# First attention of a five-block decoder: scores transposed, maxima carried as a row of the score product, sums and division moved behind the weighing of the values

## What is computed

```python
q = einsum('bsd,hdk->bhsk', x, w_q)        # 16 heads, head width 64; k and v alike
scores = einsum('bhqk,bhmk->bhqm', q, k) / 8
weights = softmax(scores, axis=-1)          # rows of 1024
z = einsum('bhqm,bhmk->bhqk', weights, v)
z = z.transpose(0, 2, 1, 3).reshape(b, s, 1024) @ w_o
x = layernorm(x + (x + z))
```

## Time and profile before

| | |
|---|---|
| median of three runs | 2817.43 us |
| profiled execution, its time | 2820.84 us |
| profiled execution, its span | 2819.0 us |
| PE busy | 2588.2 us, 92% of the span |
| DVE busy | 1811.0 us, 64% |
| ACT busy | 1525.7 us, 54% |
| POOL busy | 313.3 us, 11% |
| granted TensorE clock, mean | 0.959 |
| PE in the chain that ended last | 82% |

### The profile page before, as it was taken

One profiled execution on the slowest core, in us unless ns is written; L12 is line 12 of the kernel. 1 busy time (PEld: TensorE's weight loads), 2 busy tenths in 40 slices (PEclk: granted clock), 3 DMA queues, 4 the chain that ended last, 5 costly groups with the idle time before them and its releaser, 6 DMA issues.

```text
span 2819.0 us, 41456 instructions
## 1 busy us (share of the span) xinstructions
PE 2588.2 (92%) x16256; PEld 1902.5 (67%) x16256; DVE 1811.0 (64%) x3522; ACT 1525.7 (54%) x2551; POOL 313.3 (11%) x195
## 2 busy tenths in 40 slices
PE   7999999899999979899999999997999999986662
PEld 6666666766666668788888888996555555554421
DVE  4777774477777554777533444346887777847978
ACT  5777775477777624344444444442666555642332
POOL 0000000000000050101210222001110000004323
PEclk9999999999999989899999999998999999997886
DMA  2000000000000020000100010003222222201000
GB/s 69 16 20 12 16 20 1 19 14 22 12 12 20 1 95 18 31 1 15 47 10 22 31 43 1 8 1 74 65 65 65 65 65 61 61 2 39 1 1 30
DMA packets 47474, 82.37 MB, mean 29 GB/s; under 512 B 9512, under 2 KB 28336, under 8 KB 47280
## 3 DMA queue, kind: packets, MB, share of 16 engines
q1 hardware_dynamic: 47136, 79.65, 11.0%
q10 hardware_dynamic: 144, 0.07, 0.0%
HBM read 36.44 MB, written 2.10 MB: 14 GB/s over the span
## 4 chain that ended last, share of the span: by engine, by line
PE 82%; DVE 12%; ACT 2%; issue 2%; POOL 1%; DMA 1%; SPq 0%; DVEq 0%; ACTq 0%
PE PS L85 71%; PE PS L362 9%; DVE m_gl L921 2%; DVE s_nm L1347 1%; DVE x_E L1746 1%; DVE x_rd L1730 1%; DVE st_s L229 1%; DVE x_sm L1751 1%; DVE X L268 1%; POOL f_H L1952 1%; ACT a_KH L404 0%; PE PS L1803 0%; DMA a_wr<-in_w_v 0%; PE PS L698 0%; DVE f_w L1317 0%
## 5 line engine op out<-in xcount | busy, mean ns | idle before, releaser
L921 DVE TENSOR_TENSOR m_gl<-m_g,m_gh 128x512 fp32r<-128x512 f32 x288 | 258.1, 902 | 386.5 <-ACT m_g L760 386.5
L757 ACT ACTIVATE m_gh<-PS,cols 128x512 fp32r<-128x512 f32 x288 | 198.4, 689 | 469.9 <-PE PS L85 469.9
L483 DVE TENSOR_REDUCE a_nm<-PS 128x1 f32<-128x1024 f32 x256 | 313.5, 1225 | 210.0 <-PE PS L85 207.9
L1347 DVE TENSOR_REDUCE s_nm<-PS 128x1 f32<-128x512 f32 x512 | 344.8, 688 | 70.8 <-PE PS L85 68.2
L426 ACT ACTIVATE a_PT<-PS 128x512 f32<-128x512 f32 x512 | 278.2, 595 | 138.4 <-PE PS L362 136.7
L1264 ACT ACTIVATE s_P<-PS 128x1024 f32<-128x1024 f32 x256 | 262.0, 1024 | 164.7 <-PE PS L85 164.1
L85 PE MATMUL PS<-m_w2h,m_gh 128*128 128x256 f32 x1152 | 324.9, 282 | 18.8 <-DVE m_gl L921 18.6
L85 PE MATMUL PS<-m_w2l,m_gh 128*128 128x256 f32 x1152 | 323.5, 281 | 0.0
L85 PE MATMUL PS<-m_w2h,m_gl 128*128 128x256 f32 x1152 | 323.3, 281 | 0.0
L434 ACT ACTIVATE a_P<-PS,a_nm 128x1024 f32<-128x1024 f32 x256 | 286.1, 1117 | 16.0 <-DVE a_nm L483 15.8
L362 PEld LDWEIGHTS PS<-ident,a_P 128*128 128x128 f32 x2048 | 220.7, 141 | 96.4 <-issue 93.1
(11 more groups left out here) (295 smaller groups left out, 4441.7 us busy)
## 6 DMA issues: line engine op xcount, KB each, us to landing
m_raw<-in_m_w SPq DMA_DIRECT2D x16, 1024.0 KB, 5.1
s_Q<-s_T SPq DMA_DIRECT2D x128, 128.0 KB, 2.4
s_K<-s_T SPq DMA_DIRECT2D x128, 128.0 KB, 2.4
a_KH<-a_KH SPq DMA_DIRECT2D x56, 128.0 KB, 2.3
a_wr<-in_w_qk SPq DMA_DIRECT2D x16, 256.0 KB, 2.9
X<-in_x SPq DMA_DIRECT2D x4, 512.0 KB, 6.3
a_wr<-in_w_v SPq DMA_DIRECT2D x8, 256.0 KB, 2.7
m_raw<-in_c_w SPq DMA_DIRECT2D x2, 1024.0 KB, 8.8
```

What stands on the lines that cost most here:

```text
L483: e.tensor_reduce(a_nm[:, m:m + 1], PS[:, SB[t % 2]:SB[t % 2] + 2, :], AX.XY, ALU.max, negate=True).then_inc(s["a_max"], 1)
L757: e.activation(m_gh[r][:, :], PS[:, 4 + n % 3, :], func, bias=cols[:, bcol:bcol + 1]).then_inc(s["m_gh"], 1)
L921: e.tensor_tensor(m_gl[r][:, :], m_g0[r][:, :], m_gh[r][:, :].bitcast(F32), ALU.subtract).then_inc(s["m_gl"], 1)
L1347: e.tensor_reduce(nm2[:, n % 2, i, half:half + 1], PS[:, half, :], AX.X, ALU.max, negate=True).then_inc(s["s_nr"], 1)
```

## The change

- **Layout.** The scores are computed transposed: 128 keys stationary, 1024 queries moving. The exponentials then lie with the keys on the partitions, which is how the weighing of the values reads them, so the transposes and `a_PT` go. The weighing takes the exponentials of one tile of keys for all 1024 queries: two products of 512 columns a turn, eight turns (one head) into bank 6.
- **Maxima.** They must be known before the transposed scores. A natural product (`natural`, queries stationary, high keys only, two products of 512 columns into banks 0 and 1) is made for each of the 16 tiles of queries of the next pair, and DVE reduces it (`maximum`). After 16 of them PE turns the 128 by 16 maxima (`rows_turned`), ACT copies them (`max_rows`, `a_mh`), and SP's two DMAs lay each head's 1024 values as one row of a new tile `QM` that also holds the high queries; the matching row of `KL` is set to one by POOL. The second score product (`KL` by `QM`) so adds the negated maximum.
- **Exponentials** take no bias and give no sum. ACT writes one tile of a ring of five (`a_P`).
- **Sums.** POOL adds up the eight tiles of a head (seven additions of 128 by 1024). PE multiplies the result with a tile of ones (`totals`, 64 rows by 512, bank 7), DVE takes the reciprocal there (two of 128 by 256 for each half) and multiplies the weighed values in `a_Z` by it (`inverse`).
- **Order.** The natural products of the next pair stand in slots 4 to 13 of the 16 of a pair, two in slots 4, 5, 7, 9, 11 and 13; projections of the next pair in slots 0 to 3, keys first; totals of the pair before in slots 5 and 10; the turning in slot 14. The first pair's natural products stand among the blocks of values. Keys come before queries, and the first pair's projections before the values; for the second batch they come before the first batch's output product. The value weights are split by POOL into four tiles, the value and output weights share space with the ring, so that SP loads them after a batch's last weighing and addition.

The core of the diff (left out: the list of semaphores, the same edits of names in the second self-attention, and loops that only change indices):

```diff
-        a_P = [sb(c, f"a_P{i}", [128, S]) for i in range(4)]
-        a_PT = [sb(c, f"a_PT{i}", [128, 8, 512]) for i in range(2)]
+        N_P = 5
+        a_P = sb(c, "a_P", [128, N_P, S])
+        a_wo = a_P[:, 3:5, :].rearrange("p a (c n) -> p (a c) n", n=D)
+        a_wv = a_P[:, 0:2, :].rearrange("p a (c n) -> p (a c) n", n=512)
+        a_sum = [sb(c, f"a_sum{i}", [128, S]) for i in range(4)]
...
+        VW = [QS[1][0], QS[1][1], KH[1][0], KH[1][1]]
+        NAT_B = (4, 5, 7, 9, 11, 13)
+        def maxima_at(t):
+            first = [0]
+            for x in range(4, 14):
+                first.append(first[-1] + 1 + (x in NAT_B))
+            return range(first[t - 4], first[t - 3]) if 4 <= t < 14 else range(0)
...
         def pe_l0(e):
+            def natural(n, m):
+                i, a = m // 2, m % 2
...
+                if 16 * n + m:
+                    e.wait_ge(s["a_max"], 16 * n + m)
+                for half in range(2):
+                    t = mm(e, PS[:, half, :], QS[n % 2][a][:, i * 128:(i + 1) * 128],
+                           KH[n % 2][a][:, half * 512:half * 512 + 512], True, True)
+                t.then_inc(s["a_n"], 1)
+            def rows_turned(n):
+                e.wait_ge(s["a_max"], 16 * n + 16)
+                e.transpose(PS[0:16, 0, 0:128], a_nm[:, n % 2, :], ident[:, :]).then_inc(s["a_rw"], 1)
+            def weigh(g):
...
+                for q in range(2):
+                    t = mm(e, PS[64 * q:64 * q + 64, 6, :], a_V[:, k, h * 64:h * 64 + 64],
+                           a_P[:, g % N_P, q * 512:q * 512 + 512], k == 0, k == 7)
+            def totals(n, half, bk):
+                e.wait_ge(s["a_add"], 14 * (n + 1))
+                for a in range(2):
+                    t = mm(e, PS[64 * a:64 * a + 64, bk, :], a_one[:, :],
+                           a_sum[2 * (n % 2) + a][:, half * 512:half * 512 + 512], True, True)
+                t.then_inc(s["a_dn"], 1)
...
+                for v in range(32):
...
+                    if v % 3 != 1 and m < 16:
+                        natural(n0, m)
+                        m += 1
+                    if v == 25:
+                        rows_turned(n0)
+                for x in range(N_G):
+                    g, n, t = N_G * b + x, n0 + x // 16, x % 16
...
+                    if t == 0:
+                        e.wait_ge(s[f"row{n % 2}"], 32 * (n // 2 + 1))
...
+                        e.wait_ge(s["a_exp"], g - 1)
+                    for w, x_ in ((KH, QS), (KL, QM)):
+                        for half in range(2):
+                            ins = mm(e, PS[:, 2 + 2 * (g % 2) + half, :], w[n % 2][a][:, ks],
+                                     x_[n % 2][a][:, half * 512:half * 512 + 512], w is KH, w is KL)
+                    ms = list(maxima_at(t)) if nxt else []
+                    if ms:
+                        natural(n + 1, ms[0])
+                    if nxt and t == 14:
+                        rows_turned(n + 1)
+                    if x % 2 and x >= 3:
+                        weigh(g - 3)
+                        weigh(g - 2)
+                    if nxt and t < 4:
+                        if t:
+                            e.wait_ge(s["a_low"], 4 * (n + 1) + t)
...
+                        proj(n + 1, t, 7)
+                    if x >= 16 and t in (5, 10):
...
+                        totals(n - 1, t // 10, 7)
+                    if len(ms) > 1:
+                        natural(n + 1, ms[1])
...
         def act_l0(e):
+            def proj(n, u, bk):
...
+                    if u < 2:
+                        ins = e.activation(KH[i][a][R[a], cs], PS[R[a], bk, :], ACT.Copy)
+                    else:
+                        ins = e.activation(QS[i][a][R[a], cs], PS[R[a], bk, :], ACT.Copy, scale=0.125)
+                if u >= 2:
+                    for a in range(2):
+                        ins = e.activation(QM[i][a][R[a], cs], PS[R[a], bk, :], ACT.Copy, scale=0.125)
+                ins.then_inc(s["a_qk"], 1)
...
+                for x in range(N_G):
+                    e.wait_ge(s["a_s"], g + 1)
+                    if g >= N_P:
+                        f = g - N_P
+                        e.wait_ge(s["a_pv"], f + 1)
+                        e.wait_ge(s["a_add"], 7 * (f // 8) + max(f % 8, 1))
+                    e.activation(a_P[:, g % N_P, :].rearrange("p (h n) -> p h n", h=2),
+                                 PS[:, 2 + 2 * (g % 2):4 + 2 * (g % 2), :], ACT.Exp).then_inc(s["a_exp"], 1)
+                    if x % 8 == 1 and x > 8:
+                        emptied(g // 8 - 1)
+                    if n + 1 < n0 + 8:
+                        if t < 4:
+                            proj(n + 1, t, 7)
+                        if t == 14:
+                            max_rows(n + 1)
...
         def dve_l0(e, own):
+            def maximum(n, m):
+                i, a = m // 2, m % 2
+                e.wait_ge(s["a_n"], 16 * n + m + 1)
...
+                e.tensor_reduce(a_nm[:, n % 2, 8 * a + i:8 * a + i + 1], PS[:, 0:2, :], AX.XY, ALU.max,
+                                negate=True).then_inc(s["a_max"], 1)
+            def inverse(n, half, bk):
+                for c in range(2):
+                    r = PS[:, bk, c * 256:c * 256 + 256]
+                    e.wait_ge(s["a_dn"], 2 * n + half + 1)
+                    e.reciprocal(r, r).then_inc(own.sem, 1)
...
+                e.tensor_tensor(z, z, PS[:, bk, :], ALU.mult).then_inc(s["a_nz"], 1)
...
+                    if nxt and 1 <= t <= 4:
+                        low(n + 1, t - 1, 7)
+                    if nxt:
+                        for m in maxima_at(t):
+                            maximum(n + 1, m)
+                    if x >= 16:
+                        if t in (6, 14):
+                            quotient = inverse(n - 1, t // 14, 7)
+                        if t in (6, 8, 9, 14, 15):
+                            pump([quotient], 2 if t == 15 else 1)
...
         def pool_l0(e):
+                for x in range(N_G):
+                    g, n, k = N_G * b + x, 8 * b + x // 16, x % 8
+                    if k:
+                        e.wait_ge(s["a_exp"], g + 1)
...
+                        e.tensor_tensor(o[:, :], a_P[:, (g - 1) % N_P, :] if k == 1 else o[:, :], a_P[:, g % N_P, :],
+                                        ALU.add).then_inc(s["a_add"], 1)
+                    if x % 16 == 7 and n % 8 < 7 and n + 2 < 16:
+                        weights(n + 2)
...
         def sp_l0(e):
+                if n < 15:
+                    e.wait_ge(s["a_wp"], 2 * n + 2)
+                    e.dma_start(a_wr[:, :], A["w_qk"][(n + 1) % 8]).then_inc(s["a_wr"], 16)
+                e.wait_ge(s["a_mhd"], n + 1)
+                for a in range(2):
+                    e.dma_start(QM[i][a][ROW[a], :].bitcast(F32),
+                                a_mh[8 * a:8 * a + 8, i, :].bitcast(F32)).then_inc(s[f"row{i}"], 16)
```

More of the change, by code:

```diff
@@ L381, in act_l0, with turned @@
         def act_l0(e):
-            R = [slice(0, 64), slice(64, 128)]
-            for b in range(B):
+            def turned(b):
                 for i in range(4):
@@ new lines, in first_pair, with max_rows, emptied @@
+            def first_pair(n):
+                for u, bk in enumerate((7, 6, 3, 2)):
+                    proj(n, u, bk)
+            def max_rows(n):
+                e.wait_ge(s["a_rw"], n + 1)
+                if n >= 2:
+                    e.wait_ge(s[f"row{n % 2}"], 32 * (n // 2))
+                e.activation(a_mh[:, n % 2, :], PS[0:16, 0, 0:128], ACT.Copy).then_inc(s["a_mhd"], 1)
+            def emptied(h):
+                p, a = (h // 2) % 8, h % 2
+                e.wait_ge(s["a_pv"], 8 * h + 8)
+                if h == 16:
+                    e.wait_ge(s["a_y"], 8)
+                for q in range(2):
+                    e.activation(a_Z[R[a], p, q * 512:q * 512 + 512], PS[R[q], 6, :], ACT.Copy).then_inc(s["a_z"], 1)
@@ new lines, in first_pair @@
+            def first_pair(n):
+                for u, bk in enumerate((7, 6, 3, 2)):
+                    low(n, u, bk)
+            def maximum(n, m):
+                i, a = m // 2, m % 2
+                e.wait_ge(s["a_n"], 16 * n + m + 1)
+                if m == 0 and n >= 2:
+                    e.wait_ge(s["a_rw"], n - 1)
+                e.tensor_reduce(a_nm[:, n % 2, 8 * a + i:8 * a + i + 1], PS[:, 0:2, :], AX.XY, ALU.max,
+                                negate=True).then_inc(s["a_max"], 1)
@@ new lines, in dve_l0 @@
+            e.memset(a_one[:, :], 1.0)
+            e.wait_ge(s["a_wr"], 16)
+            e.tensor_copy(a_wh[:, :], a_wr[:, :]).then_inc(s["a_wp"], 1)
+            e.wait_ge(s["a_wp"], 1)
+            e.tensor_tensor(a_wl[:, :], a_wr[:, :], a_wh[:, :].bitcast(F32), ALU.subtract).then_inc(s["a_wp"], 1)
+            turned(0)
+            first_pair(0)
+            for b in range(B):
+                n0 = 8 * b
+                for m in range(16):
+                    maximum(n0, m)
+                    pump(slow, 1)
```

(13 more changed lines are left out.)

439 lines of the change are left out of this document (209 added, 230 removed).

## The result

The changed kernel takes **2947.5 us** (median of four runs, 2943.2 to 2950.2) against 2815.8 for the kernel before in the same comparison: ratio 1.046, 95% interval 1.043 to 1.049, slower by 132 us. The forecast was slower, 2912 us, range 2858 to 2965. The medians differ by 132 because this execution was the lowest of its four, and the profiled one before (2820.8) lay above its median.

The account below looks back on a forecast made before the run. PE was taken to bound both attention loops; a pair goes from 53 to 59.7 us, the stage is 65.5 + 446 + 88.7 + 446 + 44 = 1090, 85 over 1005, plus 10 for the clock: 2912 us, range 2858 to 2965.

Parts of the forecast that it names:

- Waits: PE's stalls in a head pair, 13.6 us: maxima, projections 2 and 3, turn 4, reciprocals, and the DMA of the maxima row.
- turn 4: PE's second natural product there waits for the first maximum, behind the low part of projection 3: 3.9 us lost, the longest.
- The nine waits of 0.55: Natural products with only scores between wait for the reduce of the single maxima buffer: 0.55 us at nine places, 5.0 a pair.
- the 46.1 us of work: PE's work in a pair: scores 14.7, natural products 7.4, values 13.9, projections 5.6, totals 1.7, changes between product kinds 2.8.
- Reciprocals: DVE's 256-column reciprocals of 1.8 us at turns 6 and 8 cost PE 0.6 us each at turns 7 and 9.
- Clock: PE's clock falls after the idle of turn 4 in two thirds of 14 pairs, at 1.1 us: 10 us.
- Start, middle, end: Outside the loops: first scores at 65.5 us (before 51), middle 88.7 (83), end 44 (42).
- POOL bounds it: Rival: sums of 3.04 us on POOL lengthen the last pair by 12 us and sometimes hold the ring; +30, 2942; chance 0.08.
- The three terms of its low end: Low end 2858: cheap reciprocal -14 us, no fall of the clock -10, 2 us a pair less of waiting -28.
- Covered: Rival at the natural products: reduce and PE overlap, bank-7 chain hides, a pair near 50 us, 49 less, 2770; chance 0.08.
- The wide value products: Rival: they do not run side by side, PE needs 0.87 us more a turn, some 200 us, 3110; chance 0.03.
- fall more than once: Rival: PE's idle stretches of 1.9, 1.2 and 3.7 us drop the clock repeatedly every pair, 48 us not 10, 2950; chance 0.07.

Follow-up runs that it names:

- Experiments 2 to 4: Three single edits, each on the changed kernel: projections over banks 7, 0, 1, 7, 2894.3 us; first maximum before the low part, 2912.8; QM copied after the signal, 2896.1.
- experiment 5: Changed kernel with projections over banks 7, 0, 1, 7, first maximum before the low part of projection 3, and QM copied after the signal, together: 2861.0 us.
- Experiment 7: Changed kernel with each 128 by 256 reciprocal replaced by a copy in place, the division left out: 2940.0 us.
- experiment 8: Changed kernel with six of POOL's seven additions of a head on 64 columns instead of 1024: 2937.7 us.
- experiment 6: Changed kernel with the projection banks, turn 4 order and later QM edits, plus maxima reduced by halves with a signal for each bank: 2798.4 us.
- experiment 3: Changed kernel with DVE taking the first maximum of turn 4 before the low part of projection 3: 2912.8 us.
- experiment 4: Changed kernel with ACT signalling after the two high parts of the queries and making QM afterwards from QS instead of PSUM: 2896.1 us.
- experiment 2: Changed kernel with the next pair's projections in banks 7, 0, 1, 7 instead of 7 four times: 2894.3 us.
- experiment 1: Changed kernel with each reduce reading 8 columns of each bank instead of 512, most of the maximum left out: 2838.9 us.
- the fastest one: Changed kernel with all four edits (projection banks, turn 4 order, later QM, halves) and second natural products at turns 5, 7, 9, 11, 12, 13: 2776.5 us, ratio 0.984.

## Why the prediction was right, and where it was too low

The direction, the place and the mechanism held; the size was short by 27 us in the profiled execution (95 forecast, 122 measured) and by 37 in the medians. By the steps:

- **Waits.** Forecast 13.6 a pair. Projections 1.9 and 1.2, turn 4 3.9, row 0.3, together 7.3: the brackets are 1.77, 1.14, 3.81 and 0.34, and with the part inside modelled ends 7.5. Experiments 2 to 4 removed each by its own cause. The second product of turn 4 starts 5.34 us after projection 3 ends (269.83 to 275.17; 5.3 forecast). The nine waits of 0.55 are eight, 4.5 in all (5.0 forecast): the ninth, from turn 4 to 5, is covered by PE's own slow clock. The reduce is 1.22 as forecast.
- **The step that was mis-sized: the 46.1 us of work.** From start to start, without the stalls and at the full clock, a pair holds 47.4 us of work, 1.3 more; experiment 5, whose clock stays full, gives nearly the same, 47.3 (55.4 less 7.7 of stalls and 0.4 for the reciprocals). The term in it that was short is the 2.8 for changes between kinds of products. Eight weighing passes take 1.87 (256.56 to 258.43) and not 1.74, and the first product behind a weighing, behind totals or behind a wait is followed by the next after 0.34, not 0.23 (258.43 to 258.77; 283.60 to 284.18 is 0.58 for two, 282.12 to 282.58 is 0.46); there are some nineteen such places in a pair. That is also why natural products stand 2.05 apart and not 1.95.
- **Reciprocals.** The duration was right (1.76 us, forecast 1.8), the cost was not: 1.2 forecast, and the two weighing groups at turns 6 and 8 pass 2.08 and 2.03 instead of 1.87, 0.4 in all, so the term is 0.8 too high. The walk let the push of 1.15 reach the product behind it and forgot that weighings stand between. Experiment 7 shows it: pairs the same within 0.2 us. The Trainium skill, VectorE: DVE Perf Modes, "Walkthrough: the 8-slice pipeline in each mode", led to an estimate of 2.13; the row says 1.76, and the measurement decides.
- **Clock.** 0.7 a pair forecast, from falls in two pairs of three at 1.1 each. It fell in every one of the 14 pairs, 17 times in all. In the pair shown the stretch of 275.95 to 279.3 us has a granted clock of 0.50, and from 275.74 to 281.55 PE took 1.5 more than at the full level. Of this 0.6 lies where the ninth wait would have been; 0.8 came on top.
- So 60.4 a pair with the clock forecast; + 0.2 and - 0.5 for the waits, + 1.3 for the work, - 0.8 for the reciprocals and + 0.8 for the clock make the measured 61.4. Errors of either sign cancel here: that the pair came out within 1.0 is in part luck.
- **First pair.** Forecast 57, measured 60.3. Two waits were forgotten: projection 1 waits 1.80 as projection 2 does, because no weighings stand ahead of it in turn 1, and without totals in turn 10 the maxima meet there too (0.66). In the first loop the clock fell twice in it, the first time behind this wait of 1.80.
- **Loop** 461, with 446 + 5 for the clock forecast: 3.3 of the first pair, 6 times 1.0, and 1.0 in the second, which took 62.4 and in which the clock also fell twice.
- **Start, middle, end** are 3.5, 3.4 and 3.3 longer than forecast; the first two were not followed further. Of the end, 3.7 is a wait for POOL that had no place in the sum: an addition of 1024 columns takes 2.37 us, not the 1.91 taken. The row it was taken from is another kind of operation: L1777 subtracts 16 values, each spread over 64 columns, and does not read two full tiles. Rows of two full tiles stood in the trace before, this one among them: 1.27 us for 512 columns, and 4.80 (L983) for 2048.

```profile
L1952 POOL TENSOR_TENSOR f_H<-f_H,f_sil 128x512 f32<-128x512 f32 x12 | 15.2, 1266 | 30.0 <-ACT f_H L1851 30.0
```

  Seven additions are 16.6 us against PE's 15.7 for a head, so POOL falls behind in the last pair, where PE has nothing else to do. The rival "POOL bounds it" had this mechanism, with 3.04; it does not hold in the loops (experiment 8). The output product takes 30.5, 0.8 over the forecast 29.7.
- **The sum of the stage.** It is 30 us over the forecast of 85 + 10: 20 in the two loops and 10 in start, middle and end. The untouched stages behind gave 3 back.
- **The range.** The three terms of its low end add up to 52, which is 2860 and not 2858; nothing hangs on it.
- **Rivals.** "Covered" did not happen because 1.38 us of PE between maxima cannot hide a cycle of 2.05; experiment 6 shows that it becomes true once the cycle is split by banks. The wide value products do run side by side (8 passes in 1.87). The clock does not fall more than once in an ordinary pair, though the gaps of 1.77 and 1.14 stand there; three of the 14 pairs had two falls, the extra one just behind a gap of about 1.80.

## What to carry to other kernels

When work leaves the engine that bounds a kernel, walk one period and compare the work left between two uses of each single buffer with that buffer's whole cycle (write, signal, read, signal back); here 5.6 us of PE work left in a pair, 12.1 us of stalls came, and slow clock and reciprocals took 1.9 more. The waits were not the price of the idea but of its buffers: a signal for each bank, free banks for the projections, the shorter dependence first in a queue, and copies that nobody waits for put after the signal turned 1.046 into 0.984. And a stall is worth more than its bracket: here 0.17 hidden in the modelled end and 0.11 at the restart on top of 0.38. A price is to be taken from a row of the same form of operation: the addition on POOL was priced from a row that reads one full tile, not two.

## What was not expected of the hardware

- A restart costs 0.11 us beside the stall: the second of two equal 512-column products starts 0.34 after the first when the first came out of a wait, 0.23 in a dense run. The same 0.34 stands behind a weighing with no wait (258.43 to 258.77).
- How long PE idles does not alone tell whether the clock falls. Behind 1.81 us it fell in experiment 3 (in the work that followed, near 256.3) and not in experiment 4. Behind 2.62 the products kept the full level (experiment 4), behind 2.75 they began at half (1.22 for two, experiment 1). Behind 3.80 they began at half in experiment 2, and behind 3.81 in the pair shown above the first two were at the full level and the fall came 0.8 us into the work.
- POOL's operations on two full fp32 tiles follow the number of columns: 0.32 us for 64 (experiment 8), 1.27 for 512 (f_H by f_sil), 2.37 for 1024. It stays 2.37 to 2.38 in the changed kernel, in the fastest one and with six of seven additions shortened. The 512 columns of a_wl took 1.53 beside DVE's division and take 1.28 in the changed kernel, where that division is gone. With the second operand 16 values spread over the columns, 1024 columns take 1.91. The two forms were not tried on the same tiles, so the form as the cause is argued from these rows.
- The exponential of 1024 columns, which no longer takes a maximum as bias nor makes a sum, takes 1.025 us instead of 1.12; which of the two does it wasn't tried apart.
